# Who spreads the values of the cross-attention layer: bias row by a TensorE product and copies on ScalarE, in place of two VectorE sums

## The chip, the cores and the metric

The kernel runs on one core of a Trainium2 chip. A core has five engines, each with an instruction queue of its own that is worked off in order: TensorE (PE, matrix products, with its weight loads shown as PEld), VectorE (DVE), ScalarE (ACT), GpSimd (POOL), and SyncE (SP), which here only issues transfers. They wait for one another by semaphores. The metric is the device time of one execution in microseconds (us).

## The reference

A decoder block over 16 sequences of 128 tokens and 128 features, 16 heads of 8 features: causal self-attention without projections, cross-attention with a context and a full bias, and a third layer with self-attention and a mixture of experts. The second layer is the one that the change touches; its values are `v`:

```python
q = (hidden_states @ Wq.T + bq) * scaling
k = key_value_states @ Wk.T + bk
v = key_value_states @ Wv.T + bv
...
scores = jnp.einsum('bhtd,bhsd->bhts', q, k) + bias
probs = jax.nn.softmax(scores, axis=-1)
attn = jnp.einsum('bhts,bhsd->bhtd', probs, v)
...
return attn @ Wo.T + bo
```

## The kernel before, in words

All five engines run the same list of slots, `for b in range(SLOTS)`. The 48 units of attention work are numbered 0 to 47: 0 to 15 are the 16 sequences in the self-attention layer, 16 to 31 the same in the cross layer, 32 to 47 in the third ("FFN"). In slot b the exponentials of unit b are taken; the scores of unit b + 2 are made ahead, to find their row maxima, the outputs of unit b - 1 are summed, and those of b - 2 are turned and divided. Two units form a pair q = b // 2; what is made once per pair (normalising, transposes, projections) is made two to four slots ahead. So there is no scheduler: the order on each engine is the order in which the functions are called in that engine's block, and what is told of the order here can be read in the calls.

Scores live in six score banks of PSUM (`pair_banks`, in three pairs that are used in turn), everything else goes through two banks, `work` and `small`. Before PE writes a bank, `claim` waits until its last reader has let go of it.

The values of pair q + 2 of the cross layer are made in even slots b, with q = b // 2, from slot 12 to slot 26: eight pairs. Before the change:

- PE, `v_products` (def at L665): two products of `hT` and the weights `w_xv` into the bank `small`. In slots 12 and 14 they stand last in their group, behind `out_transposed(b - 2)`, whose bank DVE has to let go with `att` (L1246). From slot 16 they stand between the second half of the scores, `cross_scores(b, 1)`, and `add_outputs(b - 1)` (32-column products of `probs` and `vaug` into `work`).
- DVE, `take_values` (def at L1179, instruction at L1185): two sums, one per sequence, of the bank and the bias row that is spread over all partitions in `rows`, written to `vaug` in pieces of 8 features. They stand between the two halves of `row_maxes(b + 2, ...)`: a half is a sum `biased` of scores and bias (L1200) and a maximum `rowmax` (L1207). POOL then subtracts the maxima (L455).
- ACT in an even slot of the cross layer: first exponential (L1016), issue of a bias load, second exponential, `normalise(q + 3)` (two instructions to `xn`, L975), `take_out(b - 1)` (copy to `outT`, L1022), `take_attT` (L1026), `take_hT` (L991).
- PE goes on after `add_outputs` with `attention_transposed`, `transposes(q + 3)` (of `xn`, into `work`, so behind `take_out`), `out_projected`, and in the next slot `score_maxes(b + 3)`, whose banks DVE reads with the first `biased` of that slot.

In the self layer (slots 0 to 15) DVE also adds the causal mask to the second half of the scores (L1222) before ACT can take that half's exponential.

Of the kernel before, what the change touches and what calls it, by code (L numbers as in the profile page):

```python
# [7 lines left out]
B, S, D = 16, 128, 128  # L8
# [77 lines left out]
def build(nc, a, out):  # L86
# [4 lines left out]
    with ctx:  # L91
# [55 lines left out]
        gate_b = sb("gate_b", [128, E])  # L147
        rows_out = sb("rows_out", [128, B, WIDTH])
# [80 lines left out]
        s_vp = sem("v_products")  # L229
        s_vself = sem("self_v_ready")  # L230
# [395 lines left out]
        def _(pe):  # L626
# [38 lines left out]
            def v_products(q):  # L665
                cross = player(q) == CROSS
                name, bk = ("small", small) if cross else ("work", work)
                claim(name)
                for s in range(2):
                    last = mm(bk[:, s * S:(s + 1) * S], hT[:, 1 if cross else 0, s * S:(s + 1) * S],  # L670
                              wx["xv" if cross else "fv"][:])
                last.then_inc(s_vp, 1)
                let_go[name] = s_v, q - CROSS_PAIR + 1
# [292 lines left out]
        def _(act):  # L966
# [42 lines left out]

            def exponentials(b, half):  # L1010
                if layer(b) == SELF and half == 1:
                    act.wait_ge(s_masked, b + 1)
                else:
                    act.wait_ge(s_e, 2 * b + half + 1)
                wait(act, s_pv, b - 1)
                nc.scalar.activation(probs[:, b % 2, 2 * half:2 * half + 2, :], pair("exp", b, half), ACT.Exp,  # L1016
                                     scale=1.0 if layer(b) == CROSS else SCALE).then_inc(s_p, 1)
# [42 lines left out]
            for b in range(SLOTS):  # L1060
# [12 lines left out]
                if b < FIRST_FFN:  # L1073
                    exponentials(b, 1)
                    if b in NORMED_AT:
                        normalise(NORMED_AT[b])
                    elif b % 2 == 0:
                        normalise(q + 3)
# [51 lines left out]
        def _(dve):  # L1130
# [48 lines left out]
            def take_values(q):  # L1179
                dve.wait_ge(s_vp, q - CROSS_PAIR + 1)  # L1180
                wait(dve, s_pv, 2 * q - 6)
                row = rows[:, 0 if player(q) == CROSS else 2, :]
                bk = small if player(q) == CROSS else work
                for s in range(2):
                    last = nc.vector.tensor_tensor(vaug[:, (2 * q + s) % NVAUG, :, 0:3:2, 0:HD],  # L1185
                                                   bk[:, s * S:(s + 1) * S].rearrange("p (h i d) -> p h i d", i=2, d=HD),
# [180 lines left out]
            for b in range(SLOTS):  # L1367
# [19 lines left out]
                if b == 4:  # L1387
                    nc.vector.memset(maxparts[:], 0.0).then_inc(s_dve_const, 1)
                    nc.vector.memset(ones[:], 1.0).then_inc(s_dve_const, 1)
# [26 lines left out]
                if b % 2 == 0 and CROSS_PAIR <= q + 2 < NP and b < FIRST_FFN:  # L1416
# [86 lines left out]
```

## Time and profile before

| | us |
|---|---|
| median of 3 runs | 390.37 |
| lowest, highest | 387.54, 391.88 |
| the profiled execution | 386.37 |
| its span, first to last instruction | 384.6 |
| mean granted TensorE clock | 0.941 |

Busy time over the span, of the page: PE 302.4 us (79%), its weight loads 202.4 (53%), DVE 260.6 (68%), ACT 196.9 (51%), POOL 253.5 (66%). The busy share says how full an engine is over all stages; what ends last in a stage is read from the chain of waits and the timelines. In the chain that ended last PE has 45% of the span, DVE 20%, POOL 12%, ACT 5%, and 14% is "issue", time in which an engine waited for nothing that the profile shows. The self layer takes about the first 90 us, the cross layer lasts to about 190, the third layer's attention to about 310, and the experts take the rest.

The times of the rows below are us from the start of the span, durations are us; a timeline row can merge several instructions (x2, x8), and what stands in brackets is the idle time of the engine ahead of it and who ended it. "f32" products appear as two records each, so "x4" is two products.

### The profile page before, as it was taken

How to read it: one execution, taken by the hardware profiler on the slowest of the kernel's cores; microseconds unless marked ns; L12 is line 12 of the kernel's file. 1: busy time of each engine (PE TensorE's matmuls, PEld its weight loads, DVE VectorE, ACT ScalarE, POOL GpSimd, SP SyncE). 2: the span in 40 equal slices, each digit the busy share in tenths (PEclk: the TensorE clock that was granted, in tenths of full speed). 3: DMA queues.
4: the chain of work that ended last, by engine and by line, in shares of the span. 5: the costliest groups of instructions: out<-in, count | busy, mean ns of one | idle time of the engine just before them, and what ended most of it. 6: DMA issues, size and time to landing. Idle time of an engine off the chain costs nothing.

```text
span 384.6 us, 10145 instructions
## 1 busy us (share of the span) xinstructions
PE 302.4 (79%) x3449; PEld 202.4 (53%) x3458; DVE 260.6 (68%) x665; ACT 196.9 (51%) x388; POOL 253.5 (66%) x363
## 2 busy tenths in 40 slices
PE   1869777767888999998698978788888940499993
PEld 0334334334666666666454545444444630499993
DVE  5448745487999898999446556576676655177872
ACT  3756856443555455655444736655546720155551
POOL 7875444156799889899986965687743556045554
PEclk9989999996999999999989999999999975599997
DMA  6039999200678888742111999634000102255100
GB/s 177 16 110 292 374 302 333 75 15 1 187 164 211 174 214 172 198 66 29 22 15 19 235 320 314 234 141 146 27 22 9 59 27 82 82 143 145 33 30 4
DMA packets 69186, 50.19 MB, mean 130 GB/s; under 512 B 36093, under 2 KB 50816, under 8 KB 69136
## 3 DMA queue, kind: packets, MB, share of 16 engines
q1 hardware_dynamic: 54960, 21.18, 23.0%
q10 hardware_dynamic: 12672, 25.20, 21.3%
q0 software_dynamic: 1504, 3.16, 2.4%
q8 instruction: 29, 0.48, 0.5%
q14 instruction: 21, 0.17, 0.1%
HBM read 28.48 MB, written 21.50 MB: 130 GB/s over the span
## 4 chain that ended last, share of the span: by engine, by line
PE 45%; DVE 20%; issue 14%; POOL 12%; ACT 5%; DMA 2%; SPq 0%; POOLq 0%; ACTq 0%; DVEq 0%
PE pair_banks L628 27%; PE work_bank L628 8%; DVE biased L1200 5%; PE pair_banks L631 4%; DVE pair_banks L1222 3%; DVE rowmax L1215 3%; ACT xn L975 3%; PE work_bank L631 2%; POOL biased L455 2%; POOL q_lane L432 2%; PE small_bank L631 2%; DVE att L1246 2%; DVE rowsum_inv L1240 2%; POOL rstd L409 1%; POOL routed_rows L510 1%
## 5 line engine op out<-in xcount | busy, mean ns | idle before, releaser
L1016 ACT ACTIVATE probs<-pair_banks 128x1024 f32<-128x1024 f32 x96 | 98.0, 1025 | 61.5 <-PE pair_banks L631 36.8
L455 POOL TENSOR_TENSOR biased<-biased,rowmax 128x1024 f32<-128x1024 f32 x32 | 60.5, 1897 | 16.5 <-DVE rowmax L1207 16.3
L628 PE MATMUL work_bank<-probs,vaug 128*32 128x128 f32 x1472 | 51.2, 281 | 1.4 <-DVE vaug L1185 1.2
L1215 DVE TENSOR_REDUCE rowmax<-pair_banks 128x8 f32<-128x1024 f32 x32 | 38.9, 1216 | 13.0 <-PE pair_banks L628 12.8
L628 PEld LDWEIGHTS work_bank<-probs,vaug 128*32 128x32 f32 x1472 | 38.5, 112 | 15.1 <-issue 8.1
L1200 DVE TENSOR_TENSOR biased<-pair_banks,bias_in 128x1024 f32<-128x1024 f32 x32 | 38.8, 1213 | 8.5 <-PE pair_banks L628 5.1
L521 POOL DMA_INDIRECT out<-biased x23 | 22.6, 984 | 32.6 <-DVE biased L1351 30.4
L628 PE MATMUL pair_banks<-k_lane,qT 32*128 32x512 f32 x256 | 38.3, 669 | 4.8 <-DVE biased L1200 2.5
L628 PE MATMUL pair_banks<-q_lane,kT 32*128 32x512 f32 x256 | 38.2, 668 | 3.1 <-DVE biased L1200 1.7
L631 PEld LDWEIGHTS pair_banks<-ident,biased 128*128 128x128 f32 x256 | 29.7, 149 | 18.7 <-issue 13.6
L1207 DVE TENSOR_REDUCE rowmax<-biased 128x8 f32<-128x1024 f32 x32 | 38.8, 1214 | 0.5
L631 PE MATMUL pair_banks<-ident,biased 128*128 128x128 f32 x256 | 37.4, 293 | 1.7
L1222 DVE TENSOR_TENSOR pair_banks<-pair_banks,causal 128x1024 f32<-128x1024 f32 x16 | 19.6, 1227 | 17.7 <-PE pair_banks L628 17.6
L1022 ACT COPY outT<-work_bank 128x256 f32<-128x256 f32 x46 | 17.0, 369 | 26.2 <-PE work_bank L628 25.9
L432 POOL TENSOR_TENSOR k_lane<-kT,in_lane 128x1024 f32<-128x1024 f32 x16 | 30.3, 1893 | 0.0
L975 ACT ACTIVATE xn<-x_sb,shift,rstd 128x128 f32<-128x128 f32 x48 | 20.9, 486 | 9.4 <-POOL shift L414 9.4
L628 PE MATMUL pair_banks<-xn,probs 128*128 128x128 f32 x184 | 25.7, 287 | 0.0
L628 PE MATMUL pair_banks<-bias_in,probs 128*128 x184 | 24.9, 278 | 0.1
L628 PEld LDWEIGHTS pair_banks<-xn,probs 128*128 128x128 f32 x184 | 23.9, 204 | 0.0
L510 POOL DMA_INDIRECT routed_rows<-rows_out,position_i x16 | 16.2, 1012 | 11.3 <-DVE position_i L1293 8.0
L432 POOL TENSOR_TENSOR q_lane<-kT,in_lane 128x1024 f32<-128x1024 f32 x8 | 15.1, 1892 | 11.7 <-ACT kT L999 8.9
L628 PEld LDWEIGHTS pair_banks<-bias_in,probs 128*128 128x128 f32 x184 | 22.3, 191 | 0.7 <-issue 0.3
(193 smaller groups left out, 552.6 us busy)
## 6 DMA issues: line engine op xcount, KB each, us to landing
routed_rows<-cleared SPq DMA_DIRECT2D x8, 1028.0 KB, 14.3
routed_rows<-cleared ACTq DMA_DIRECT2D x8, 1028.0 KB, 6.8
bias_in<-in_w SPq DMA_DIRECT2D x16, 256.0 KB, 9.2
biased<-routed_rows SPq DMA_DIRECT2D x23, 128.5 KB, 2.1
ctx_in<-in_ctx SPq DMA_DIRECT2D x8, 128.0 KB, 6.5
att_scratch<-att SPq DMA_DIRECT2D x16, 64.0 KB, 5.2
att_rows<-att_scratch SPq DMA_DIRECT2D x16, 64.0 KB, 4.4
x_sb<-in_x SPq DMA_DIRECT2D x1, 640.0 KB, 5.0
```

The source lines that it names most:

```text
L432: return nc.gpsimd.tensor_tensor(dst, src.unsqueeze(1).to_broadcast([128, G, PAIR]), in_lane[:].unsqueeze(2).to_broadcast([128, G, PAIR]), ...
L455: nc.gpsimd.tensor_tensor(v, v, rowmax[:, b % 2, 8 * half:8 * half + 8].unsqueeze(2).to_broadcast([128, 8, S]), ALU.subtract).then_inc(s_s ...
L510: nc.gpsimd.indirect_dma_start(out=routed, out_offset=bass.IndirectOffsetOnAxis(ap=position_i[:, n:n + 1], axis=0), in_=rows_out[:, n, :], ...
L521: nc.gpsimd.indirect_dma_start(out=out.rearrange("b s d -> (b s) d"), out_offset=bass.IndirectOffsetOnAxis(ap=tile_rows[:, i, 2 * D:WIDTH] ...
L628: return nc.tensor.matmul(o, lhsT, rhs, start=start, stop=stop, **kw)
L631: return nc.tensor.matmul(o, src, ident[:], start=True, stop=stop, is_transpose=True)
L975: last = nc.scalar.activation(xn[:, i, s, :], x_sb[:, first + s, :], ACT.Identity, bias=shift[:, i, s:s + 1], scale=rstd[:, i, kind, s:s + 1])
L1016: nc.scalar.activation(probs[:, b % 2, 2 * half:2 * half + 2, :], pair("exp", b, half), ACT.Exp, scale=1.0 if layer(b) == CROSS else SCALE ...
L1200: nc.vector.tensor_tensor(biased[:, i, two, :], banks, bias_in[:, b % NBIAS, 8 * half:8 * half + 8, :].rearrange("p (g h) k -> p g (h k)", ...
L1207: nc.vector.tensor_reduce(peak, biased[:, i, two, :].rearrange("p g (h k) -> p (g h) k", k=S), AX.X, ALU.max).then_inc(s_rmax, 1)
L1215: nc.vector.tensor_reduce(peak, banks.rearrange("p g (h k) -> p (g h) k", k=S), AX.X, ALU.max).then_inc(s_mfree, 1)
L1222: nc.vector.tensor_tensor(banks, banks, causal[:].rearrange("p g k -> p (g k)").unsqueeze(1).to_broadcast([128, 2, G * S]), ALU.add).then_ ...
```

## The change

In the cross layer only, the bias row is added on PE: behind each of the two value products a second product with one row of weights (`ones_row`, a new tile [1, 128] of ones) and one moving row (`rows[0:1, 0, :]`, the bias row as partition 0 has it) accumulates into the same bank. ACT then copies the bank to `vaug`, two copies, called behind the second exponential and ahead of `normalise`. DVE's sums remain for the third layer's pairs, whose place is unchanged. DVE gets one more memset, in slot 4, and PE waits for it with a semaphore of its own.

```diff
@@ -145,6 +145,7 @@
+        ones_row = sb("ones_row", [1, S])
@@ -227,6 +228,7 @@
+        s_row = sem("ones_row_ready")
@@ -666,9 +668,14 @@
                 claim(name)
-                for s in range(2):
-                    last = mm(bk[:, s * S:(s + 1) * S], hT[:, 1 if cross else 0, s * S:(s + 1) * S],
-                              wx["xv" if cross else "fv"][:])
+                if cross:
+                    pe.wait_ge(s_row, 1)
+                for s in range(2):
+                    o = bk[:, s * S:(s + 1) * S]
+                    last = mm(o, hT[:, 1 if cross else 0, s * S:(s + 1) * S], wx["xv" if cross else "fv"][:],
+                              stop=not cross)
+                    if cross:
+                        last = mm(o, ones_row[:], rows[0:1, 0, :], start=False)
                 last.then_inc(s_vp, 1)
                 let_go[name] = s_v, q - CROSS_PAIR + 1
@@ -1007,6 +1014,15 @@
+            def take_values(q):
+                act.wait_ge(s_vp, q - CROSS_PAIR + 1)
+                wait(act, s_pv, 2 * q - 6)
+                act.wait_ge(s_dve_const, 2)
+                for s in range(2):
+                    last = nc.scalar.copy(vaug[:, (2 * q + s) % NVAUG, :, 0:3:2, 0:HD],
+                                          small[:, s * S:(s + 1) * S].rearrange("p (h i d) -> p h i d", i=2, d=HD))
+                last.then_inc(s_v, 1)
+
@@ -1072,6 +1088,8 @@
                 if b < FIRST_FFN:
                     exponentials(b, 1)
+                    if b % 2 == 0 and CROSS_PAIR <= q + 2 < FFN_PAIR:
+                        take_values(q + 2)
                     if b in NORMED_AT:
                         normalise(NORMED_AT[b])
                     elif b % 2 == 0:
@@ -1179,11 +1197,10 @@
             def take_values(q):
                 dve.wait_ge(s_vp, q - CROSS_PAIR + 1)
                 wait(dve, s_pv, 2 * q - 6)
-                row = rows[:, 0 if player(q) == CROSS else 2, :]
-                bk = small if player(q) == CROSS else work
+                row = rows[:, 2, :]
                 for s in range(2):
                     last = nc.vector.tensor_tensor(vaug[:, (2 * q + s) % NVAUG, :, 0:3:2, 0:HD],
-                                                   bk[:, s * S:(s + 1) * S].rearrange("p (h i d) -> p h i d", i=2, d=HD),
+                                                   work[:, s * S:(s + 1) * S].rearrange("p (h i d) -> p h i d", i=2, d=HD),
                                                    row.rearrange("p (h i d) -> p h i d", i=2, d=HD), ALU.add)
                 last.then_inc(s_v, 1)
@@ -1386,6 +1403,7 @@
                     nc.vector.memset(maxparts[:], 0.0).then_inc(s_dve_const, 1)
+                    nc.vector.memset(ones_row[:], 1.0).then_inc(s_row, 1)
                     nc.vector.memset(ones[:], 1.0).then_inc(s_dve_const, 1)
@@ -1413,7 +1431,7 @@
-                if b % 2 == 0 and CROSS_PAIR <= q + 2 < NP and b < FIRST_FFN:
+                if b % 2 == 0 and FFN_PAIR <= q + 2 < NP and b < FIRST_FFN:
                     take_values(q + 2)
```

The first place that the prediction speaks of is ACT's queue in slot 26, the last of the eight. Before (L975 `xn`, L1022 `outT`, L1026 `attT`, L993 `hT`):

```order
L1016 ACTIVATE probs<-pair_banks 128x1024
L1037 DMA bias_in<-in_bias 128x16x128
L1016 ACTIVATE probs<-pair_banks 128x1024
L975 ACTIVATE xn<-x_sb,shift,rstd 128x128 x2
L1022 COPY outT<-work_bank 128x256
L1026 COPY attT<-small_bank 128x128
L993 ACTIVATE hT<-work_bank,cols 128x256
```

The same place with the change (line numbers are those of the changed file):

```order
L1032 ACTIVATE probs<-pair_banks 128x1024
L1053 DMA bias_in<-in_bias 128x16x128
L1032 ACTIVATE probs<-pair_banks 128x1024
L1022 COPY vaug<-small_bank 128x8x2x8 x2
L982 ACTIVATE xn<-x_sb,shift,rstd 128x128 x2
L1038 COPY outT<-work_bank 128x256
L1042 COPY attT<-small_bank 128x128
L1000 ACTIVATE hT<-work_bank,cols 128x256
```

The two copies stand between the exponential and `xn`; everything behind them keeps its order. The second place is PE's queue in the same slot, from the second half of the scores to the transposes. Before:

```order
L631 MATMUL pair_banks<-ident,biased 128x128 x8
L628 MATMUL small_bank<-w_xv,hT 128x128 x2
L628 MATMUL work_bank<-probs,vaug 32x128 x16
L631 MATMUL small_bank<-ident,att_rows 128x128
L631 MATMUL work_bank<-ident,xn 128x128 x2
```

With the change:

```order
L633 MATMUL pair_banks<-ident,biased 128x128 x8
L630 MATMUL small_bank<-w_xv,hT 128x128
L630 MATMUL small_bank<-rows,ones_row 128x128
L630 MATMUL small_bank<-w_xv,hT 128x128
L630 MATMUL small_bank<-rows,ones_row 128x128
L630 MATMUL work_bank<-probs,vaug 32x128 x16
L633 MATMUL small_bank<-ident,att_rows 128x128
L633 MATMUL work_bank<-ident,xn 128x128 x2
```

Each value product is followed by its one-row product, ahead of `add_outputs`.

## Rows read from the trace of the kernel before

**Rows 1.** Window: us, busy of PE, PEld, DVE, ACT, POOL; clock, DMA share, GB/s.
```profile
128.47:141.41 12.94, 12.03 (x139) 8.63 (x142) 11.88 (x21) 7.25 (x15) 11.62 (x11) 1.00 0.84 193
```

**Rows 2.** Chain in order of time (start, us, what): slots 20, 24, 26.
```profile
122.88 0.87 ACT xn L975 x2
...
145.43 1.24 DVE biased L1200
...
161.70 0.87 ACT xn L975 x2
```

**Rows 3.** Timelines of PE, DVE and ACT, slot 24.
```profile
146.71 1.09 PE L631 MATMUL pair_banks<-ident,biased 128*128 128x128 f32 x8
147.64 0.61 PE L628 MATMUL small_bank<-w_xv,hT 128*128 128x128 f32 x4
148.18 1.08 PE L628 MATMUL work_bank<-probs,vaug 128*32 128x128 f32 x32
...
149.94 0.44 PE L631 MATMUL work_bank<-ident,xn 128*128 128x128 f32 x2 [0.42 <-ACT outT L1022]
...
148.28 0.49 DVE L1185 TENSOR_TENSOR vaug<-small_bank,rows 128x128 f32<-128x128 f32 x2
148.69 1.21 DVE L1200 TENSOR_TENSOR biased<-pair_banks,bias_in 128x1024 f32<-128x1024 f32 x1
...
151.98 1.23 DVE L1200 TENSOR_TENSOR biased<-pair_banks,bias_in 128x1024 f32<-128x1024 f32 x1 [0.63 <-issue]
...
147.84 1.02 ACT L1016 ACTIVATE probs<-pair_banks 128x1024 f32<-128x1024 f32 x1 [0.41 <-PE pair_banks L631]
148.76 0.87 ACT L975 ACTIVATE xn<-x_sb,shift,rstd 128x128 f32<-128x128 f32 x2
149.53 0.35 ACT L1022 COPY outT<-work_bank 128x256 f32<-128x256 f32 x1
149.78 0.27 ACT L1026 COPY attT<-small_bank 128x128 f32<-128x128 f32 x1
```

**Rows 4.** Timelines of PE and ACT, slots 12 and 14.
```profile
65.42 0.71 PE L628 MATMUL small_bank<-w_xv,hT 128*128 128x128 f32 x4 [0.67 <-DVE att L1246]
66.89 0.44 PE L631 MATMUL work_bank<-ident,xn 128*128 128x128 f32 x2 [0.77 <-ACT outT L1022]
...
78.60 0.71 PE L628 MATMUL small_bank<-w_xv,hT 128*128 128x128 f32 x4 [0.68 <-DVE att L1246]
80.07 0.44 PE L631 MATMUL work_bank<-ident,xn 128*128 128x128 f32 x2 [0.76 <-ACT outT L1022]
...
81.58 1.14 PE L628 MATMUL pair_banks<-k_lane,qT 32*128 32x512 f32 x8 [0.85 <-DVE biased L1200]
...
65.72 0.86 ACT L975 ACTIVATE xn<-x_sb,shift,rstd 128x128 f32<-128x128 f32 x2
66.48 0.35 ACT L1022 COPY outT<-work_bank 128x256 f32<-128x256 f32 x1
...
79.67 0.35 ACT L1022 COPY outT<-work_bank 128x256 f32<-128x256 f32 x1
```

**Rows 5.** Timelines of PE and ACT, slot 16.
```profile
96.45 0.82 PE L628 MATMUL small_bank<-w_xv,hT 128*128 128x128 f32 x4
97.20 1.08 PE L628 MATMUL work_bank<-probs,vaug 128*32 128x128 f32 x32
...
98.39 0.35 ACT L1022 COPY outT<-work_bank 128x256 f32<-128x256 f32 x1
```

**Rows 6.** Timeline of POOL, end of the cross scores' maxima.
```profile
167.73 1.90 POOL L455 TENSOR_TENSOR biased<-biased,rowmax 128x1024 f32<-128x1024 f32 x1 [0.33 <-DVE rowmax L1207]
```

**Rows 7.** Windows around the low clock, and the PE product at its start.
```profile
84.00:90.50 6.50, 3.65 (x46) 2.00 (x46) 5.00 (x11) 3.15 (x5) 3.41 (x2) 0.97 0.01 3
90.50:97.00 6.50, 6.46 (x30) 4.96 (x30) 4.38 (x6) 1.33 (x3) 4.29 (x8) 0.51 0.11 29
...
90.54 2.09 PE L628 MATMUL pair_banks<-k_lane,qT 32*128 32x512 f32 x8 [1.39 <-DVE biased L1200]
```

## What the change will do to the time

> **What bounds the kernel now.** Read first the table of windows for one pair of cross slots, 128.47 to 141.41 us: DVE is busy 11.88 of 12.94 us, PE 12.03, POOL 11.62, ACT only 7.25 [rows 1]. By busy time one would take work off DVE and give it to ACT, and that is what the change does. But the share does not say who is waited for, so the chain is read next. Through the cross stage it repeats every 12.94 us: DVE's first bias sum (145.43) frees score banks, PE fills them, ACT takes the exponentials, and then the chain stays on ACT: 0.87 us of `xn` (normalise, L975), then `outT` (take_out, L1022), and only then goes back to PE and DVE [rows 2]. The `xn` step stands in the chain in slots 20, 22, 24 and 26 at the same place (first and last shown in [rows 2]).
>
> The timeline of slot 24 shows why [rows 3]. ACT runs the second exponential at 147.84, `xn` at 148.76 and `outT` at 149.53 with no idle time. PE waits 0.42 us for that `outT` before it may put the next transposes into the work bank (149.94), behind them stand the output projection and the maximum scores, and DVE's next bias sum (151.98) starts only with those, after 0.63 us idle. DVE's values sums (148.28, next instruction 148.69: 0.41 us a pair) lie earlier in that slot, and their time is followed by idle time. So DVE is nearly full, yet in even slots it waits; ACT is half empty, yet is waited for.
>
> **The change part by part.** Eight pairs are touched (slots 12, 14, ..., 26).
>
> *DVE loses* 8 x 0.41 = 3.3 us. In slot 24 it would reach the bias sum of 151.98 with 0.63 + 0.41 us idle instead of 0.63. Worth nothing where PE is late, which is so in every slot below. The one-row memset that DVE gains, once, in slot 4, has no row of its own; a memory set of one partition costs at most what the 0.28 us sum of 128 partitions costs, and at that point DVE waits for PE as a rule: nothing, at most 0.3.
>
> *PE gains* two one-row products a pair. No row shows one. The two value products that stand there take 147.64 to 148.18, so 0.27 us each [rows 3]. Bounds: 0.14 us, the transposes of 146.71 (eight in 1.09 us, the cheapest full-width instruction), and 0.38 us, the same value products where the clock is low (96.45 to 97.20, two) [rows 5]. I take 0.27, since they have the same 128 columns, the same type and a weight load of their own. That is 0.54 us a pair ahead of add_outputs, and also ahead of the semaphore on which the values are taken.
>
> *ACT gains* two copies of 128x128 a pair out of PSUM, between the second exponential and `xn`. The nearest row is the copy to `attT` at 149.78, same size and source, 0.27 us [rows 3]. Instructions of ACT overlap: `outT` is 0.35 us long but the next one starts 0.25 us later (149.53, 149.78), 0.10 less. So a copy costs 0.17 in a queue, two 0.34; upper bound 0.54, no overlap (and the cut-up output address costs DVE nothing: 0.49 us for two). By the Trainium skill, "ScalarE: Activation LUTs", section What ACT_TABLE_LOAD costs, an activation with immediates takes 186 ns + 0.833 ns per element and overlaps the next by 93 ns, so an estimate of 0.20 us a copy; the row gives 0.17, and by the page the sum below would be 0.5 us larger. The same page's Rules for kernel authors would leave a plain sum on VectorE; by duration alone the trace sees no difference (0.28 on DVE, 0.27 on ACT), so that rule tells nothing of the place in the queue.
>
> Behind the new wait on ACT are queued `xn`, `outT`, `attT` and `hT`, and PE waits for the first two of these. Slot by slot:
>
> Slots 18 to 26 (five), by slot 24: the value products end at 147.64 + 0.61 = 148.25, now at 148.79; with 0.04 for the hand-over ACT may start at 148.83, 0.07 after it is free (148.76). Delay of `outT`: 0.07 + 0.34 = 0.41. PE's add_outputs now ends at 148.18 + 0.54 + 1.08 = 149.80, before the new start of `outT` at 149.94, so PE's own addition is hidden under ACT's. If the copies were free it would show with up to 0.27. 5 x 0.41 = 2.05; bounds 0.34 (no wait) and 0.83 (0.29 wait, 0.54 copies).
>
> Slot 12: the products wait for DVE's `att`, start at 65.42 and end at 66.13, while ACT goes on with `xn` at 65.72 [rows 4]. Now ACT waits for 66.13 + 0.54 + 0.04 = 66.71, copies until 67.05, and after 0.76 for `xn` starts `outT` at 67.81 instead of 66.48: 1.33. PE waited 0.77 for that `outT`, and the next self scores stand behind it: all of it counts. Bounds 1.07 and 1.75.
>
> Slot 14: `outT` moves by the same reckoning from 79.67 to 81.01 and PE's transposes from 80.07 to 81.41; they end 0.66 later, at 82.1. Before, the maximum scores behind them waited 0.85 for DVE and began at 81.58 [rows 4]. So 0.5 of the delay is left; DVE being 0.4 earlier helps no more, as it is no longer what PE waits for. Bounds 0.25 and 0.93.
>
> Slot 16: products end at 96.45 + 0.82 = 97.27, + 0.54 + 0.04 + 0.34 + 0.77 gives 98.96 against 98.39 [rows 5]: 0.57. Bounds 0.31 and 0.99.
>
> Sum: 1.33 + 0.50 + 0.57 + 2.05 = 4.45 us; bounds 3.3 and 7.8. Does it last? After slot 26 DVE hands over to POOL at 167.73, where POOL had been idle 0.33 [rows 6], so POOL has no backlog to absorb a delay in; from there POOL, then PE and the tail run as before, only later. Odd slots hold none of the changed work. The profiled execution took 386.37 us: 386.4 + 4.45 = 390.8. The median of three is 390.37, so 394.8 there, slower by 1.15%.
>
> **The rivals.**
>
> *DVE sets the pace after all (not slower).* If the first bias sum of each pair were reached by DVE's own queue, the 0.41 us would come back eight times: 386.4 - 3.3 = 383.1 (387.1 by the median). For it: 11.88 of 12.94 us busy. Against it: the 0.63 us idle in front of that very sum. It decides only if ACT's `outT` could take 0.34 us of copies without moving, which needs add_outputs to end after `xn` does; it ends at 149.26 against 149.53. 6%.
>
> *The copies are mostly hidden (no change).* PE's products near 0.14 us, copies that cost less than 0.17, and slot 12 absorbed by waits that the trace does not show: 0 to +2 us, 388. 8%.
>
> *The clock, one low stretch more.* TensorE ran at the lower of its levels, 1.2 GHz (granted 0.51), from 90.5 to 97, after a wait of 1.39 us at the end of a stretch in which it was busy 3.65 of 6.5 us [rows 7]. PE was busy 6.46 us in it, half of which would be saved at 2.4 GHz: 3.2 us a stretch. The change makes PE wait 1.6 us in slot 12 and again in 14 where it waited 0.8. One more: 386.4 + 4.45 + 3.2 = 394.0 (398.0). 10%. The Trainium skill, "TensorE: Matmul & The Clock Gate", Part 1, says that idle time brings the lower clock and that its timing varies from run to run; the trace agrees on the first, and no row tells the second.
>
> *The clock, one low stretch less.* The added products and the shift in time could as well spare the stretch at 90.5: 386.4 + 4.45 - 3.2 = 387.6 (391.6). 8%.
>
> The forecast keeps 68%.
>
> **How the numbers follow.** About 1% (3.9 us) is what a measurement of this kernel can tell from no change. The forecast's 4.45 lies just above, its bounds are 3.3 and 7.8 and the upper is far off: I give it two in three to be over 1%, so 0.44; with the extra low stretch 0.54 slower. Same: 0.24 + 0.08 + 0.08, and a third of the DVE case, 0.42. Faster: 0.04. Range on the scale of the median: the low end takes in most of the spared stretch and some of the hidden case, 389.5; the high end the upper bound with a little margin and the extra stretch, 399.
>
> **What would show it.** In the profile after: `vaug<-small_bank` copies on ACT of 0.27 us between exponential and `xn`; in slot 24's place `outT` some 0.4 us later relative to the exponential; a cross pair of 13.35 us instead of 12.94; DVE busy 3.3 us less but idle more, with over 1 us in front of the even slots' last bias sum; PE idle about 1.6 us in slot 12 before the transposes. One-row products near 0.14 us or over 0.38, a low clock stretch gained or lost, or an unchanged period would make the forecast wrong.

## The result and the profile after

| | before | after |
|---|---|---|
| median, us | 388.96 (4 runs, 386.75 to 391.88) | 397.69 (4 runs, 396.26 to 401.26) |
| ratio | 1 | 1.0234, interval 1.0127 to 1.0341 |
| the profiled execution, us | 386.37 | 396.26 |
| its span, mean granted clock | 384.6, 0.941 | 394.5, 0.942 |

The change costs 8.7 us by the medians and 9.9 us between the two profiled executions. Slower was the forecast and 397.69 lies in its range, but its sum was 4.45 us: half of the loss was not in it, and the upper bound of that sum, 7.8, is exceeded too. That the median comes within 2.9 us of the 394.8 forecast is partly luck: it was added to a median of 390.37 from three executions, and 53 later ones of the kernel before average 388.15.

First the page of after, its part 1, the clock line of its part 2 and the shares of the chain that ended last:

```profile
PE 312.4 (79%) x3481; PEld 206.3 (52%) x3490; DVE 257.6 (65%) x650; ACT 200.7 (51%) x404; POOL 254.2 (64%) x363
...
PEclk9989989888999999999989999999999985599999
...
PE 45%; DVE 16%; POOL 15%; issue 14%; ACT 6%; DMA 2%; SPq 0%; POOLq 0%; ACTq 0%; DVEq 0%
```

DVE is 3.0 us less busy (260.6 before), ACT 3.8 us busier (196.9), PE 10.0 us busier (302.4). DVE's share of the chain has fallen from 20% to 16%, and nothing was gained. In the stretch where the change begins, the clock line has its low places in slices 8 to 10 (69 to 99 us); the one deep place of before, in slice 10, is spread over three shallower ones.

The steady part of the cross stage is read from the window of one pair, from the step of the chain of waits into the products of the bank `small` (slot 20) to the same step a pair later, in the columns of [rows 1]:

```profile
128.64:142.47 13.83, 13.05 (x140) 9.29 (x139) 11.55 (x19) 7.71 (x17) 11.82 (x12) 1.00 0.80 181
```

A pair takes 13.83 us against 12.94 [rows 1], at the full clock in both: 0.89 us more, where 0.41 was forecast. DVE is 0.33 us less busy, PE 1.02 us busier. The chain of waits of after shows what stands in the added time (start, us, what; slot 22, which runs at the full clock like slot 24 of [rows 2, 3]):

```profile
142.47 1.48 PE small_bank L630 x8
...
144.13 0.27 ACT vaug L1022
144.41 0.77 ACT xn L982 x2
145.18 0.27 ACT outT L1038
```

In [rows 2] the chain went from the exponential straight to `xn`. Now PE's products into the bank `small` stand in it with 1.48 us, then the copy to `vaug`. The timeline of PE at that place answers to the PE part of [rows 3]:

```profile
142.30 0.39 PE L630 MATMUL small_bank<-w_xv,hT 128*128 128x128 f32 x2
142.62 0.48 PE L630 MATMUL small_bank<-rows,ones_row 1*128 1x128 f32 x2
143.03 0.49 PE L630 MATMUL small_bank<-w_xv,hT 128*128 128x128 f32 x2
143.45 0.48 PE L630 MATMUL small_bank<-rows,ones_row 1*128 1x128 f32 x2
143.86 1.08 PE L630 MATMUL work_bank<-probs,vaug 128*32 128x128 f32 x32
...
145.49 0.44 PE L633 MATMUL work_bank<-ident,xn 128*128 128x128 f32 x2 [0.29 <-ACT outT L1038]
```

From start to start: 0.32, 0.41, 0.42, 0.41, together 1.56 us ahead of `add_outputs`, where the two value products alone took 148.18 - 147.64 = 0.54 [rows 3]. The two one-row products add 1.02 us, not 0.54: 0.41 each for themselves, and 0.10 for each value product, which took 0.32 and 0.42 here. The weight loads show how:

```profile
142.62 0.29 PEld L630 LDWEIGHTS small_bank<-rows,ones_row 1*128 1x128 f32 x2
143.03 0.30 PEld L630 LDWEIGHTS small_bank<-w_xv,hT 128*128 128x128 f32 x2
143.45 0.29 PEld L630 LDWEIGHTS small_bank<-rows,ones_row 1*128 1x128 f32 x2
```

Each group of loads starts together with its products (142.62, 143.03, 143.45), not under the products ahead. In the kernel before, the loads of the 32-column weights of `add_outputs` are the only ones at this place that do so (they start at 148.18, with their products). ACT at the same place:

```profile
142.50 1.02 ACT L1032 ACTIVATE probs<-pair_banks 128x1024 f32<-128x1024 f32 x1 [0.41 <-PE pair_banks L633]
143.97 0.43 ACT L1022 COPY vaug<-small_bank 128x128 f32<-128x128 f32 x2 [0.45 <-PE small_bank L630]
144.29 0.88 ACT L982 ACTIVATE xn<-x_sb,shift,rstd 128x128 f32<-128x128 f32 x2
145.07 0.36 ACT L1038 COPY outT<-work_bank 128x256 f32<-128x256 f32 x1
```

`outT` starts 145.07 - 142.50 = 2.57 us after the exponential, before it was 149.53 - 147.84 = 1.69 [rows 3]: 0.88 later. The copies are 0.32 of it (143.97 to 144.29); the other 0.55 is the time from where ACT was free (142.50 + 0.92, the step from exponential to next instruction in [rows 3]) to 143.97. DVE, behind it:

```profile
146.48 0.29 DVE L1276 TENSOR_TENSOR x_sb<-small_bank,x_sb 128x128 f32<-128x128 f32 x1 [1.10 <-PE small_bank L630]
147.53 1.23 DVE L1217 TENSOR_TENSOR biased<-pair_banks,bias_in 128x1024 f32<-128x1024 f32 x1 [0.76 <-PE pair_banks L630]
```

It now stands idle for 1.86 us where it was 0.63 [rows 3]: its own 0.41 and the longer pair.

Slot 12, PE and ACT, answers to [rows 4]:

```profile
66.02 0.49 PE L630 MATMUL small_bank<-w_xv,hT 128*128 128x128 f32 x2 [0.68 <-DVE att L1263]
...
67.79 0.43 ACT L1022 COPY vaug<-small_bank 128x128 f32<-128x128 f32 x2 [1.37 <-PE small_bank L630]
68.89 0.36 ACT L1038 COPY outT<-work_bank 128x256 f32<-128x256 f32 x1
69.31 0.69 PE L633 MATMUL work_bank<-ident,xn 128*128 128x128 f32 x2 [1.55 <-ACT outT L1038]
```

From the first value product to `outT` it is 2.87 us, before 66.48 - 65.42 = 1.06 [rows 4]: 1.81 later. In slot 14 the two stand at 82.48 and 85.35 (before 78.60 and 79.67), also 1.80 more; in slot 16 at 101.10 and 103.94 against 96.45 and 98.39 [rows 5], 0.90 more. What the clock did around these slots, in the columns of [rows 7]:

```profile
69.31:72.85 3.54, 3.32 (x13) 1.51 (x14) 0.00 (x0) 0.59 (x1) 0.63 (x2) 0.56 0.46 134
86.05:90.05 4.00, 3.25 (x14) 0.84 (x13) 1.44 (x2) 0.59 (x1) 3.52 (x2) 0.57 0.11 33
96.48:100.00 3.52, 3.52 (x16) 2.01 (x17) 2.43 (x2) 0.00 (x0) 3.25 (x8) 0.54 0.00 0
```

Before there was one stretch of 6.5 us at 0.51 [rows 7]; now there are three of 3.5 to 4 us near it, of which the first two begin right behind PE's waits of 1.55 and 1.56 us for `outT`, the third behind one of 1.40 us for DVE's `biased`.

**Where the time went, slot by slot.** In both timelines I took the start of `add_outputs` in the odd slot behind each even slot (before: 68.98 behind slot 12, 85.17 behind slot 14), and subtracted before from after. The table gives how much each slot added (us), for after and for the experiments below. "12.94 becomes" is the length of a pair from slot 20 on, where it is steady.

| kernel | ahead of slot 12 | slot 12 | slot 14 | slot 16 | 18 to 26 | behind | span | 12.94 becomes |
|---|---|---|---|---|---|---|---|---|
| after | 0.61 | 3.27 | 2.07 | -0.39 | 4.70 | -0.36 | +9.9 | 13.83 |
| no bias products | 0.05 | 0.80 | -0.13 | 0.19 | 1.90 | 0.29 | +3.1 | 13.27 |
| DVE copies | 0.56 | 1.48 | 0.47 | 0.79 | 4.03 | 1.67 | +9.0 | 13.77 |
| full-row products | 0.46 | 2.79 | 0.33 | -1.85 | 2.84 | 0.93 | +5.5 | 13.27 |
| 32-row products | 0.32 | 3.64 | 3.26 | 0.83 | 4.31 | -0.16 | +12.2 | 13.83 |
| one wide product | -0.66 | 2.91 | 1.42 | -0.56 | 3.91 | 0.08 | +7.1 | 13.62 |
| slots 16 to 26 only | 0.62 | 0.00 | 0.01 | 0.77 | 4.29 | 1.01 | +6.7 | 13.83 |
| values behind `xn` | -0.67 | 2.58 | 1.55 | 1.98 | 4.40 | 1.26 | +11.1 | 13.77 |
| early `xn` | -0.61 | 0.00 | 0.95 | -1.17 | -0.16 | 1.89 | +0.9 | 12.75 |
| no DVE sums | 1.14 | 0.00 | 1.16 | 0.99 | -0.01 | -0.08 | +3.2 | 12.94 |
| the change once more | -0.09 | 3.64 | 3.26 | 0.80 | 4.68 | -0.29 | +12.0 | 13.83 |

"Behind" and "ahead" hold no changed work: over the profiles of these kernels they run from -0.36 to 1.89 and from -0.67 to 1.14, and the place of the low clock varies too. The steady length of a pair repeats to 0.01 us, so the verdicts below rest on it and on the timed medians, and a single span is read only together with its slots.

### The profile page after: what moved, and what is told of

It reads as the page before. It is cut to its first block, busy times and chain, and to the rows that moved or that the text cites. A ratio compares the mean times of both kernels' runs of the same rounds, so it can differ in the third digit from the quotient of the medians.

```text
span 394.5 us, 10218 instructions
## 1 busy us (share of the span) xinstructions
PE 312.4 (79%) x3481; PEld 206.3 (52%) x3490; DVE 257.6 (65%) x650; ACT 200.7 (51%) x404; POOL 254.2 (64%) x363
## 4 chain that ended last, share of the span: by engine, by line
PE 45%; DVE 16%; POOL 15%; issue 14%; ACT 6%; DMA 2%; SPq 0%; POOLq 0%; ACTq 0%; DVEq 0%
PE pair_banks L630 25%; PE work_bank L630 8%; POOL biased L457 5%; PE small_bank L630 4%; PE pair_banks L633 3%; DVE biased L1217 3%; ACT xn L982 3%; DVE rowmax L1232 3%; PE work_bank L633 2%; PE small_bank L633 2%; DVE pair_banks L1239 2%; DVE att L1263 2%; DVE rowsum_inv L1257 2%; POOL q_lane L434 1%; POOL k_lane L434 1%
## 5 line engine op out<-in xcount | busy, mean ns | idle before, releaser
L630 PE MATMUL pair_banks<-k_lane,qT 32*128 32x512 f32 x256 | 39.3, 686 | 3.8 <-DVE biased L1217 1.4
L630 PE MATMUL pair_banks<-q_lane,kT 32*128 32x512 f32 x256 | 39.6, 690 | 2.2 <-DVE biased L1217 1.3
L633 PEld LDWEIGHTS pair_banks<-ident,biased 128*128 128x128 f32 x256 | 28.3, 144 | 19.1 <-issue 13.6
L633 PE MATMUL pair_banks<-ident,biased 128*128 128x128 f32 x256 | 35.7, 284 | 2.1 <-DVE biased L1217 0.5
```

The costliest lines, as they stand in the source:

```text
L630: return nc.tensor.matmul(o, lhsT, rhs, start=start, stop=stop, **kw)
L633: return nc.tensor.matmul(o, src, ident[:], start=True, stop=stop, is_transpose=True)
```

## The experiments

The times, each beside runs of the kernel before on the same chip (their medians 387.83 us for the first four kernels, 387.45 for the next four and 388.78 for the last two of the table):

| kernel | median us (runs) | ratio, interval | mean clock of its runs |
|---|---|---|---|
| no bias products | 390.72 (10) | 1.0065, 1.0034 to 1.0096 | 0.940 |
| DVE copies | 395.69 (4) | 1.0192, 1.0133 to 1.0252 | 0.933 |
| full-row products | 391.2 (10) | 1.0069, 1.0036 to 1.0103 | 0.943 |
| slots 16 to 26 only | 392.71 (4) | 1.012, 1.0061 to 1.0179 | 0.939 |
| one wide product | 393.48 (1) | | 0.939 |
| 32-row products | 398.52 (1) | | 0.921 |
| values behind `xn` | 396.53 (4) | 1.0212, 1.0143 to 1.028 | 0.934 |
| early `xn` | 388.02 (12) | 1.0013, 0.9985 to 1.0042 | 0.939 |
| no DVE sums | 388.07 (10) | 0.998, 0.9946 to 1.0015 | 0.939 |
| the change once more | 397.71 (6) | 1.0225, 1.018 to 1.0269 | 0.932 |
| before, all | 388.15 mean (53) | | 0.940 |

**The two halves of the change apart.** The first kernel keeps ACT's copies and drops the bias products:

```diff
                     o = bk[:, s * S:(s + 1) * S]
-                    last = mm(o, hT[:, ...], wx["xv" if cross else "fv"][:], stop=not cross)
-                    if cross:
-                        last = mm(o, ones_row[:], rows[0:1, 0, :], start=False)
+                    last = mm(o, hT[:, ...], wx["xv" if cross else "fv"][:])
```

> The changed kernel without its one-row products: ACT still copies the bank to vaug ahead of xn, the bias row of the values is left out. Theory (the one-row products and the slower value products beside them, 1.02 us a pair more on PE, make most of the loss; the copies only cost their own 0.32 us): a cross pair takes 12.94 + 0.32 = 13.26 us, ACT does not wait ahead of the copies in slots 18 to 26, the span is near 384.6 + 8 x 0.32 + about 1 in slots 12 and 14 = 388. Rival A (moving the values to ACT's queue is what costs, whatever PE does): a pair stays near 13.83 and the span near 394. Rival B (nothing but the low clock moved): a pair of 12.94 and any span.

Its timeline of ACT in the steady part:

```profile
149.99 1.02 ACT L1029 ACTIVATE probs<-pair_banks 128x1024 f32<-128x1024 f32 x1 [0.42 <-PE pair_banks L633]
150.92 0.42 ACT L1019 COPY vaug<-small_bank 128x128 f32<-128x128 f32 x2
151.21 0.90 ACT L979 ACTIVATE xn<-x_sb,shift,rstd 128x128 f32<-128x128 f32 x2
```

No idle time ahead of the copies: PE is early enough when it has only the two value products. What the copies cost, 0.29 in the queue and 13.27 - 12.94 = 0.33 a pair, is the forecast's 0.34. The whole costs 0.65%. So the copies are not the missing half.

The second kernel keeps the bias products and gives the copies back to DVE, at the place of the old sums:

```diff
-                    if b % 2 == 0 and CROSS_PAIR <= q + 2 < FFN_PAIR:
-                        take_values(q + 2)
...
+                    if player(q) == CROSS:
+                        last = nc.vector.tensor_copy(v, small[...])
```

> The changed kernel with its one-row products, but the bank is copied to vaug by DVE, in the place where the sums stood before. Theory: ACT no longer waits for the products, but outT waits for add_outputs, which ends 1.02 us later; before it ended 0.27 us ahead of outT, so a pair takes 12.94 + 0.75 = 13.7 us, nearly the 13.83 of the changed kernel, and DVE idles more. Slots 12 and 14 lose much less than in the changed kernel, since xn does not stand behind the products: span near 384.6 + 6 x 0.75 = 389 to 390. Rival A (ACT's copies are the cost): a pair near 12.94.

Its timeline of ACT:

```profile
154.42 0.87 ACT L982 ACTIVATE xn<-x_sb,shift,rstd 128x128 f32<-128x128 f32 x2
156.01 0.37 ACT L1038 COPY outT<-work_bank 128x256 f32<-128x256 f32 x1 [0.72 <-PE work_bank L630]
```

ACT has nothing added, and yet a pair takes 13.77. `outT` now waits 0.72 us for the end of `add_outputs`, which the bias products have pushed back. Before, `add_outputs` ended 0.27 us before `outT` (149.26, 149.53 [rows 3]): 1.02 of products less these 0.27 is 0.75, and 0.83 was measured. So the two halves do not add up (0.33 and 0.83, together 0.89). In the changed kernel two ways lead to `outT`: over ACT, which waits 0.55 us more for the products and then copies for 0.32, and over PE's `add_outputs`, which by this kernel costs 0.83. The longer one counts, and they are nearly equal. The median of this kernel, 395.69, is more than its waits alone explain; its clock is low (0.933), and that is taken up at the end.

**Is it the single row, the count of the products, or their change of shape?** The next kernel gives the bias product all 128 rows: weights with ones in row 0 and zeros elsewhere, and the bias rows of all partitions as moving data. The sum is the same.

```diff
-        ones_row = sb("ones_row", [1, S])
+        first_row = sb("first_row", [128, S])
...
-                        last = mm(o, ones_row[:], rows[0:1, 0, :], start=False)
+                        last = mm(o, first_row[:], rows[:, 0, :], start=False)
```

> The changed kernel with the bias product over all 128 rows: weights whose first row is one and the others zero, moving tile the bias row on all partitions. The result is the same. Theory (the one-row product is dear because a weight load of another number of rows is not loaded under the running product, so that each product and each switch back costs 0.41 instead of 0.27): the four products take 4 x 0.27 = 1.08 us instead of 1.56, and a pair 13.83 - 0.48 = 13.35 us, the value that was forecast for the change. Rival (any added product, or accumulating into the same columns, costs 0.41): four products 1.56 us and a pair of 13.83.

Its timeline of PE:

```profile
151.55 0.39 PE L630 MATMUL small_bank<-w_xv,hT 128*128 128x128 f32 x2
151.77 0.39 PE L630 MATMUL small_bank<-rows,first_row 128*128 128x128 f32 x2
151.99 0.39 PE L630 MATMUL small_bank<-w_xv,hT 128*128 128x128 f32 x2
152.22 0.39 PE L630 MATMUL small_bank<-rows,first_row 128*128 128x128 f32 x2
152.53 1.08 PE L630 MATMUL work_bank<-probs,vaug 128*32 128x128 f32 x32
```

0.22, 0.22, 0.23 and 0.31: four products in 0.98 us where the changed kernel took 1.56, with as many products of the same columns. The expectation had still put each product at 0.27 (1.08 us, a pair of 13.35). A product with 128 times as many rows is cheaper, since it has the shape of what stands before and behind it. A pair is 13.27, as long as without any bias product, and the loss of time 0.69% in place of 2.3%. That is the mis-sized term found: of the 0.89 us a pair, 0.56 come from the change between one row and 128. The same kernel's weight loads:

```profile
151.66 0.30 PEld L630 LDWEIGHTS small_bank<-rows,first_row 128*128 128x128 f32 x2
151.88 0.30 PEld L630 LDWEIGHTS small_bank<-w_xv,hT 128*128 128x128 f32 x2
```

Here each starts 0.11 us ahead of its products (151.77, 151.99), under the ones before.

The next one asks whether it is one row as such, or any change of the number of rows. It differs from the last in two numbers:

```diff
-        ones_row = sb("ones_row", [1, S])
+        first_row = sb("first_row", [32, S])
...
-                        last = mm(o, ones_row[:], rows[0:1, 0, :], start=False)
+                        last = mm(o, first_row[:], rows[0:32, 0, :], start=False)
```

> The changed kernel with the bias product over 32 rows instead of one (first row ones, the others zero). Theory A (what is dear is the change from 128 rows of weights to another number and back, 0.41 us for each product on either side): the four products take about 1.56 us as with one row, a pair 13.83 us. Theory B (only a single row is dear): 0.22 us each as with full rows (0.89 for four), a pair 13.27.

Its timeline of PE:

```profile
144.40 0.39 PE L630 MATMUL small_bank<-w_xv,hT 128*128 128x128 f32 x2
144.72 0.48 PE L630 MATMUL small_bank<-rows,first_row 32*128 32x128 f32 x2
145.13 0.49 PE L630 MATMUL small_bank<-w_xv,hT 128*128 128x128 f32 x2
145.55 0.48 PE L630 MATMUL small_bank<-rows,first_row 32*128 32x128 f32 x2
145.97 1.08 PE L630 MATMUL work_bank<-probs,vaug 128*32 128x128 f32 x32
```

0.32, 0.41, 0.42, 0.42, that is 1.57 us, and a pair of 13.83: as with one row. It is the change of the number of rows, not the single row. The steps of the last two kernels also say where the time lies. A step with no change of shape at either end is 0.22; with a change at one end it is 0.31 or 0.32, whether rows change (the first step here) or columns (the last step with full rows, into `add_outputs`); with a change at both ends it is 0.41 or 0.42. So each change costs about 0.2 us, half of it on either side.

Then one product of 256 columns for both sequences, ahead of the two value products, which accumulate onto it. The shape changes three times up to `add_outputs` in place of four.

```diff
+                if cross:
+                    mm(bk[:, 0:2 * S].rearrange("p (s d) -> p s d", s=2), ones_row[:],
+                       rows[0:1, 0:1, :].to_broadcast([1, 2, D]), start=True, stop=False)
...
-                        last = mm(o, ones_row[:], rows[0:1, 0, :], start=False)
```

> The changed kernel with one one-row product of 256 columns, ahead of the two value products, instead of two of 128 behind each. Theory (each change of the number of rows costs one load that is not hidden, and the columns cost what they cost in other products, 0.22 for 128, 0.43 for 256): scores to wide product and wide product to value product are the only two changes, so about 0.63 + 0.22 + 0.22 = 1.1 to 1.3 us in place of 1.56, and a pair of 13.4 to 13.6 us. Rival (each one-row product costs a fixed amount, whatever stands beside it): 0.41 + 0.27 + 0.27 = 0.95 us, a pair of 13.27 to 13.3.

Its timeline of PE:

```profile
139.76 0.69 PE L630 MATMUL small_bank<-rows,ones_row 1*128 1x256 f32 x2
140.39 0.71 PE L630 MATMUL small_bank<-w_xv,hT 128*128 128x128 f32 x4
141.03 1.08 PE L630 MATMUL work_bank<-probs,vaug 128*32 128x128 f32 x32
```

1.27 us for all (0.63 and 0.64), and a pair of 13.62: 0.3 us less than four products that alternate, 0.3 more than four of one shape. The 0.64 for two value products is a change at one end of each, 0.32 twice. There was one execution, so only the steps and the length of the pair are used.

**Where in the program the loss arises.** Here pairs 8 and 9 (slots 12 and 14) keep DVE's sums, and only slots 16 to 26 are changed:

```diff
+                by_act = CROSS_PAIR + 2 <= q < FFN_PAIR
...
-                    if b % 2 == 0 and CROSS_PAIR <= q + 2 < FFN_PAIR:
+                    if b % 2 == 0 and CROSS_PAIR + 2 <= q + 2 < FFN_PAIR:
```

> The change in slots 16 to 26 only; the pairs of slots 12 and 14 are made as before (no one-row product, DVE sums). Theory: what the change costs in slots 12 and 14 goes away, by the traces 1.8 us of waiting in slot 12 and 1.5 to 2 in slot 14 and what the low clock added there: span 394.5 - 4 to 6 = 388.5 to 390.5, with a pair of 13.83 in the cross stage as in the changed kernel. Rival (the cost of slots 12 and 14 is only that of the low clock, which would come at another place): span near 394 all the same.

Slots 12 and 14 add nothing, the other six 5.1 us, and the median is 1.2% above before instead of 2.3%. So two of the eight slots carry nearly half of the loss. The span was 391.3 where 388.5 to 390.5 had been expected: 1.0 us of it was added behind the last changed slot.

**Does the place in ACT's queue matter?** The copies behind `xn` in place of ahead of it:

```diff
                     exponentials(b, 1)
-                    if b % 2 == 0 and CROSS_PAIR <= q + 2 < FFN_PAIR:
-                        take_values(q + 2)
...
                         normalise(q + 3)
+                    if b % 2 == 0 and CROSS_PAIR <= q + 2 < FFN_PAIR:
+                        take_values(q + 2)
```

> The changed kernel with ACT's two copies behind xn instead of ahead of it (and still ahead of outT). Theory (ACT waits for PE's products with xn queued behind the wait): in slots 12 and 14 xn runs during the wait and outT comes 0.76 us earlier in each; in the cross slots outT is then set by add_outputs (1.02 us later than before the change), a pair 13.7 us instead of 13.83. Together 1.5 + 6 x 0.1 = 2.1 us less than the changed kernel: ratio to before near 1.018. Rival (the place in the queue does not matter): as the changed kernel.

Its timeline of ACT:

```profile
143.17 0.87 ACT L982 ACTIVATE xn<-x_sb,shift,rstd 128x128 f32<-128x128 f32 x2
143.94 0.42 ACT L1022 COPY vaug<-small_bank 128x128 f32<-128x128 f32 x2
144.76 0.37 ACT L1038 COPY outT<-work_bank 128x256 f32<-128x256 f32 x1 [0.40 <-PE work_bank L630]
```

The copies no longer wait, `xn` fills the time. But `outT` waits 0.40 us for `add_outputs`, and a pair falls only to 13.77, the same as with the copies on DVE: PE is the limit. In slots 12 and 14, where ACT had waited 1.37 us, 0.69 and 0.52 us come back (2.58 and 1.55 in the table against 3.27 and 2.07). The profiled execution lost that again in slot 16 (1.98, where after has -0.39), and the median, 396.53, cannot be told from that of the change.

**What DVE's relief is worth.** The kernel before, with its cross sums replaced by a copy of one column:

```diff
-                row = rows[:, 0 if player(q) == CROSS else 2, :]
...
+                if player(q) == CROSS:
+                    last = nc.vector.tensor_copy(vaug[:, 2 * q % NVAUG, 0, 0, 0:1], small[:, 0:1])
```

> The kernel before, with DVE's two sums for the cross values replaced by a copy of one column (the values of the cross layer are left out), nothing added anywhere else: DVE's relief alone. Theory (DVE waits for PE in front of the even slots' last bias sum, so its 0.41 us a pair are worth nothing): a pair stays 12.94 us, the idle time ahead of that sum grows by 0.3 to 0.4, span within 0.5 us of 384.6 but for the low clock. Rival (DVE sets the pace, 11.88 of 12.94 us busy): a pair of 12.6 us and 2.5 to 3 us less in all.

Its timeline of DVE, at the place of 151.98 in [rows 3]:

```profile
142.33 1.22 DVE L1203 TENSOR_TENSOR biased<-pair_banks,bias_in 128x1024 f32<-128x1024 f32 x1 [0.76 <-PE pair_banks L628]
```

The values of the cross layer are left out here. A pair stays at 12.94 and the ratio is 0.998 (0.9946 to 1.0015). With most of that work gone, DVE waits for PE a little longer: 0.13 us more at this sum (0.3 to 0.4 had been expected), the rest in short waits before it. In the steady part there was nothing to be gained by DVE's relief.

**Is ACT's queue the chain in the kernel before as well?** If so, taking `xn` out of it must shorten a pair. Nothing is moved between engines: in the cross slots `normalise` is called ahead of the exponentials.

```diff
+                early = FIRST_CROSS <= b < FIRST_FFN and b % 2 == 0
+                if early:
+                    normalise(q + 3)
                 if b < FIRST_FFN:
```

> The kernel before, without any of the change; in the even cross slots ACT makes xn ahead of the second exponential instead of behind it, where it has 0.41 us of idle time. Theory (in even slots the chain runs over exponential, xn and outT on ACT, and add_outputs ends only 0.27 us ahead of outT): outT is then set by add_outputs, a pair 12.94 - 0.23 = 12.7 us, 1.4 us over six pairs, ratio 0.996. Rival (the second exponential, now 0.25 us later, gives it back by letting go of its banks later): a pair of 12.94 or more.

Its timeline of ACT and DVE in an even slot:

```profile
146.71 0.87 ACT L975 ACTIVATE xn<-x_sb,shift,rstd 128x128 f32<-128x128 f32 x2
147.48 1.01 ACT L1016 ACTIVATE probs<-pair_banks 128x1024 f32<-128x1024 f32 x1
148.72 0.37 ACT L1022 COPY outT<-work_bank 128x256 f32<-128x256 f32 x1 [0.23 <-PE work_bank L628]
...
151.18 1.23 DVE L1203 TENSOR_TENSOR biased<-pair_banks,bias_in 128x1024 f32<-128x1024 f32 x1 [0.43 <-issue]
```

`outT` follows the second exponential after 1.24 us instead of 1.69 [rows 3], and DVE waits 0.43 us for its sum instead of 0.63. A pair takes 12.75, 0.19 less (0.23 had been expected). More is not to be had this way, since `outT` now waits 0.23 us for the end of `add_outputs`. It confirms the chain. The time stays: 1.0013 (0.9985 to 1.0042), where 0.996 had been expected. In the profile slot 18 took about 0.6 us longer than before, which the four shorter pairs behind it only just made up (-0.16 in the table). Behind slot 26 it was ahead by 0.99 us, two slots on by 0.48, and the end came 0.9 later. Why that lead is lost was not found out. No kernel of this study is faster than before by more than the spread.

**The change once more**, for its spread and its clock:

> The changed kernel once more, with more rounds, beside the same runs of the kernel before, for a narrower ratio and a second profile. Theory (1.8 us of wait in slot 12, about 1 in slot 14, 0.6 to 0.7 in slot 16, 0.89 a pair in slots 18 to 26, so 8 us, and up to 3 us of low clock on top in some executions): the cross stage again 13.83 us a pair, ratio 1.02 to 1.03; the profile may show the low clock in other slots than the first did. Rival (the first profile's span was a chance of the clock): ratio under 1.015.

397.71 us from six executions, 396.24 to 398.38, ratio 1.0225 with the narrower interval 1.018 to 1.0269, and a pair of 13.83. In its profile slots 12, 14 and 16 add 7.7 us together, in after's 4.95. The windows of its low clock there:

```profile
67.70:74.60 6.90, 5.77 (x46) 3.11 (x48) 1.23 (x1) 3.04 (x6) 0.87 (x2) 0.51 0.39 118
84.80:101.90 17.10, 13.87 (x74) 6.67 (x76) 9.76 (x14) 4.32 (x8) 9.38 (x11) 0.50 0.03 9
```

That is 24 us at the low clock, where after had three stretches of 3.5 to 4 us and the kernel before had 6.5 [rows 7]. Some 13 us more of it than in after cost 2.75 us (7.7 less 4.95), under half of the prediction's price, which was 3.2 us for 6.5.

## Why the prediction was right, and where its sum was wrong

**Who is waited for: right.** The window said DVE, the chain said ACT. The kernel without DVE's sums keeps 12.94 us a pair, the one with an earlier `xn` has 12.75. The rival "DVE sets the pace" (6%) has fallen with both.

**The copies on ACT: right.** 0.17 each were forecast; 0.32 for two stand in after's queue (143.97 to 144.29), 0.29 in the kernel without bias products, 0.33 in its pair. The upper bound of 0.54 was far above. The rival "mostly hidden" (8%) has fallen with the same number. The estimate of 0.20 us a copy that the prediction worked out from the Trainium skill, "ScalarE: Activation LUTs", section What ACT_TABLE_LOAD costs, is a little above all of these; the measurement decides.

**The one-row product: wrong, and this is the term that carries the gap.** "The two value products that stand there take 147.64 to 148.18, so 0.27 us each": that average hides a cheap step of 0.22, to a product of the same shape, and a dear one of 0.32, to the 32-column weights of `add_outputs`. The price belongs to the change of shape between neighbours, about 0.1 us on either side of it. Before there was one change, into `add_outputs`; the new products make it four. So each one-row product cost 0.41, and each value product 0.10 more than before (0.32 in place of 0.22, and 0.42 in place of 0.32): 1.02 us for the two instead of 0.54. The upper bound, 0.38 a product, was taken from products at the low clock; 0.51 a product at the full clock, its neighbour's share included, lies above it. The prediction had named "over 0.38" as what would prove it wrong. A rule that the prediction did not use would have warned: by the Trainium skill, "TensorEngine Tiling (Array Packing)", section Key Properties, "Changing tiling mode (not just tile) drains the TensorE". The same page lists arrays of 32 rows, and of 32 columns, as modes apart from the full array; of a single row it says nothing. The runs agree that a change costs time, 0.31 to 0.42 us a step with it and 0.22 without, and that 32 columns, 32 rows and one row all count as a change; no run shows what the array does inside.

**What followed from it.** Slots 18 to 26: wait of ACT 0.55 in place of 0.07, copies 0.32, sum 0.87 in place of 0.41. The step "PE's own addition is hidden under ACT's" still held, but barely: `add_outputs` ends at 143.86 + 1.08 = 144.94, `outT` starts at 145.07, and the kernel with DVE copies shows 0.83 a pair by PE's side alone. Slot 12: 1.81 in place of 1.33, the 0.48 of PE's products more. Slot 14: 1.80 - 0.85 of waiting for DVE that was there anyway [rows 4], 0.95 in place of 0.50. Slot 16: 0.90 in place of 0.57. With the measured terms the forecast's own sum is 1.81 + 0.95 + 0.90 + 5 x 0.89 = 8.1 us in place of 4.45. The medians differ by 8.7 (after) and 8.9 (the change once more). The structure of the sum held, one price in it did not.

**The clock: neither rival as it was told.** In the two profiled executions the mean clock is the same, 0.941 and 0.942. What is left between 9.9 and 8.1 is in the table: 0.61 ahead of the first changed slot, 1.46 and 1.12 beyond the waits in slots 12 and 14, where the low clock had come in (stretches at 69.31 and 86.05), -1.29 in slot 16, where less of it was left, 0.25 in slots 18 to 26, and -0.36 behind; together 1.8. Over more executions there is a difference: the ten of the change have a mean clock of 0.931 (0.915 to 0.942), 53 of the kernel before 0.940. At equal clock, 0.939 to 0.942, the change took 396.24 to 396.46 (three executions) and before 387.3 on average (12, at 0.941 and 0.942): 9.0 us. Over all, the means are 397.8 and 388.15: 9.6. So on average a lower clock adds under 1 us, and most of the loss is waits. The price of 3.2 us for one more low stretch was too high as well: 13 us more of low clock, two such stretches, cost 2.75 us in the second profile.

**The rest.** DVE's 3.3 us (3.0), PE's idle time of 1.6 us in slot 12 (1.55) and DVE's idle time of over 1 us (1.86) came as forecast. That the delay of the cross slots stays in the end held to 0.4 us in after (10.27 us late behind slot 26, 9.9 at the end).

**What stays open.** Kernels with products of few rows in slots 12 and 14 ran at a mean clock of 0.931 to 0.934 (the change, DVE copies, values behind `xn`; the one execution with 32 rows 0.921), those without them, or with full-row ones, at 0.939 to 0.943. The one wide product with 0.939 from one execution does not fit or is chance. The longer waits of PE there are not enough to explain it: without bias products PE waits 1.55 us for `outT` in both slots (ahead of 67.74 and 81.72), the clock is 1.00 from 66 to 84, and its low stretch (0.50 from 90.2 to 97) is where the kernel before has it; with DVE copies PE's transposes of `xn` follow there without a wait (67.64 and 82.30), and the clock is low behind slot 12 all the same (0.50 from 68.3 to 71.7). Whether it is how the products are fed was not tested further. Nor was the lead tracked down that the earlier `xn` loses behind the cross stage.

## What to carry to other kernels

Before work is moved to the emptier engine, read in the chain who is waited for, and what is queued behind the new instructions there: here the full engine had idle time where it counted, and the half-empty one had none. A product is priced with its neighbours, not alone: where a bias row is added on TensorE, giving the product the same number of rows as the products around it cost 0.7% here, against 2.3% with one row. Where two ways lead to a common point, the longer one counts (0.87 over ACT and 0.83 over PE gave 0.89), so mending one of the two gives little; the full-row products shortened both.

## What the runs showed of the hardware that was not expected

A float32 product of 128 columns took 0.22 us from its start to the next one's when it had the shape of both neighbours, 0.31 to 0.32 when the shape of the weights changed at one end, and 0.41 to 0.42 when it changed at both. It made no difference whether the change was one of rows (128 to 1, 128 to 32, and back) or of columns (128 to 32). At a change the weight load starts together with its product instead of under the one ahead. The time did not depend on the number of rows itself: one row with 128 columns was dearer than 128 rows.

The low clock differs much between executions of one kernel: around slots 12 to 16 the changed kernel had three stretches of 3.5 to 4 us in one profile, and stretches of 6.9 and 17.1 us in the next, and its times ran from 396.24 at a mean clock of 0.939 to 401.26 at 0.915.
